# Mixture-of-experts stage: TensorE's program written out row by row, with its first weights addressed in place

## The reference, cut to what matters

```python
# x: layer norm of h, (32 rows, 153 tokens, 192 channels); E = 3 experts, F = 768
scores = softmax(mean(x, axis=1) @ Wg.T)
sel = top_k(scores, 1)                         # one expert per row
h1 = gelu(x @ W1[sel] + b1[sel])               # (153, 768)
y = h1 @ W2[sel] + b2[sel]                     # (153, 192)
out = h + y * scores[sel]
```

## Time and profile before

| | us |
|---|---|
| median of three executions (lowest to highest) | 1019.19 (1018.41 to 1020.95) |
| the profiled execution, its own time | 1023.18 |
| its span, from the first instruction to the last | 1021.4 |
| experts stage, first SyncE entry to the end of the span | 851.3 to 1021.4 |

### The profile page before, as it was taken

How to read it: one execution, slowest core, us unless ns; L and a number is a source line. 1 busy time by engine, 2 the same in 40 slices (tenths; PEclk the granted TensorE clock), 3 DMA queues, 4 the chain that set the end, 5 groups by cost and what they waited for, 6 DMA issues and landing times. The chain is left out here.

```text
span 1021.4 us, 23392 instructions
## 1 busy us (share of the span) xinstructions
PE 705.7 (69%) x6531; PEld 483.7 (47%) x6532; DVE 873.0 (85%) x2391; ACT 708.9 (69%) x1374; POOL 168.2 (16%) x276
## 2 busy tenths in 40 slices
PE   3783387757788376676767667666644386999997
PEld 3562144425555234343434334333323254998996
DVE  5879997988888889999999999999978874676766
ACT  0345365977888789988988998999845293554553
POOL 5851220017664100000000000000004530000000
PEclk9986598988999777878877887788757597999999
DMA  8000000001111111111111111111022004455452
GB/s 260 3 3 0 0 1 1 1 1 40 37 37 37 40 31 25 24 24 24 25 24 24 24 26 24 24 25 24 17 91 75 17 1 155 147 194 193 171 194 82
DMA packets 84274, 54.75 MB, mean 54 GB/s; under 512 B 53704, under 2 KB 83176, under 8 KB 83976
## 3 DMA queue, kind: packets, MB, share of 16 engines
q1 hardware_dynamic: 83208, 54.11, 17.4%
q0 software_dynamic: 1024, 0.13, 0.3%
HBM read 11.90 MB, written 3.76 MB: 15 GB/s over the span
## 5 line engine op out<-in xcount | busy, mean ns | idle before, releaser
L1377 DVE SCALAR_TENSOR_TENSOR expo<-expo,con,pow 128x153 f32<-128x153 f32 x480 | 146.2, 377 | 0.7 <-ACT expo L1287 0.7
L1287 ACT ACTIVATE expo<-at_rem,con 128x459 f32<-128x459 f32 x160 | 98.1, 644 | 14.7 <-PE at_rem L1160 11.2
L962 DVE TENSOR_REDUCE rs_ends<-rs_banks 128x770 f32 (+1 forms) x96 | 89.3, 957 | 12.8 <-PE rs_banks L934 10.6
L784 PE MATMUL at_banks<-pick,row_top 128*128 128x459 bf16 x160 | 73.5, 459 | 37.7 <-ACT word L1250 37.1
L1413 DVE CUSTOM_DVE_ANT_0 weight_top<-weight_top,line 128x2448 uint16<-128x2448 uint16 x64 | 85.6, 1351 | 8.1 <-ACT line L1279 6.3
L1159 PE MATMUL at_rem<-word,ident_half 128*128 128x459 f16 x160 | 64.7, 404 | 37.2 <-ACT expo L1287 34.6
L883 ACT ACTIVATE rs_banks<-rs_banks 128x770 f32<-128x770 f32 x96 | 74.6, 796 | 22.4 <-PE rs_banks L926 21.6
L1243 ACT ACTIVATE pT_all<-at_pT 128x768 bf16<-128x768 int16 (+3 forms) x160 | 79.0, 563 | 13.8 <-PE at_pT L1183 8.3
L1250 ACT ACTIVATE word<-at_banks 128x459 uint8<-128x459 f32 x160 | 79.9, 562 | 9.9 <-PE at_banks L789 8.7
L1943 ACT ACTIVATE qk<-e_p,b1s 128x153 f32<-128x153 f32 x192 | 58.9, 392 | 29.0 <-PE e_p L1904 27.8
L1904 PE MATMUL e_p<-X,qk 128*128 (+1 forms) x960 | 72.9, 236 | 7.7 <-DMA qk<-vt 6.9
(11 more groups left out here) (389 smaller groups left out, 2036.2 us busy)
## 6 DMA issues: line engine op xcount, KB each, us to landing
qk<-vt SPq DMA_DIRECT2D x64, 384.0 KB, 3.1
rs_kb<-qk SPq DMA_DIRECT2D x128, 28.7 KB, 2.0
kb<-qk SPq DMA_DIRECT2D x128, 28.7 KB
patches<-in_patches SPq DMA_DIRECT2D x4, 768.0 KB
vi<-vt SPq DMA_DIRECT2D x32, 96.0 KB, 2.0
out<-vi SPq DMA_DIRECT2D x32, 96.0 KB, 1.8
pj_w<-in_w SPq DMA_DIRECT2D x1, 2304.0 KB, 8.3
qb<-qk SPq DMA_DIRECT2D x128, 6.0 KB
```

The lines of the kernel that those rows point to most:

```text
L784: pe.matmul(bank[:, 0:3 * N], top, pick[:, 3 * i:3 * i + 3, :].rearrange("p w n -> p (w n)"), start=True, stop=False, skip_group_check=True)
L962: v.tensor_reduce(ends[:, :, n, 5 * b:5 * b + 5], banks[:, slot(u, b), :, 0:5 * W].rearrange("p i (t n) -> p i t n", n=W), AX, ALU.max).th ...
L1287: act.activation(bank(ex, b), rem[:, (u + b) % 2, 0:3 * N], ACT.Square, scale=2.0 ** 24, bias=c(5)).then_inc(sq_done, 1)
L1377: ins = v.scalar_tensor_tensor(ex[:, t, :], ex[:, t, :], c(7), pw[:, t, :].bitcast(BF16), ALU.add, ALU.mult, accum_out=tot[:, t:t + 1])
```

## The change

The ring of first weights goes. TensorE's program is written out for all 32 rows, so that the row number is a constant in it; the first product reads `w1h` and `w1l` where they lie, at an address that depends on the expert's register, and the expert number is read one row ahead. SyncE instead copies the expert's low second weight `w2l` (`wl`, a slot of four) and its bias (`bias2`) for each row, and waits for the end of the collect of row n-4 (`i_bias`) before it refills a slot. The image part of the second product is written as six pairs: `w2h` into partitions 0 to 63 of `p3`, `wl` into partitions 64 to 127. VectorE no longer reads the expert number, waits for the row's copies (`w_in`), and has one more addition for the image rows. ScalarE's program, SyncE's and VectorE's loops stay.

```diff
@@ -1828,7 +1828,10 @@
         sb = lambda n, s, t=F32: k.sb(n, s, t, st)
         g = m["qkflat"][:, 12288:12288 + 4 * FT * N].bitcast(F32).rearrange("p (u f n) -> p u f n", u=2, f=FT)
         gs = sb("e_gs", [P, 2, FT, N + 32 + NT], BF16)
-        ws = m["qkflat"][:, 0:SLOTS * 4 * FF].rearrange("p (s i a f) -> p s i a f", s=SLOTS, i=2, a=2)
+        bias2 = m["pj_raw"][:, :, :].rearrange("p a b -> p (a b)")[:, 0:SLOTS * C].rearrange("p (u c) -> p u c", u=SLOTS)
+        wl_own = sb("e_w2_low", [P, 2, FT, C], BF16)
+        wl_line = m["line"][:, :, :].rearrange("p a b -> p (a b)")[:, 2 * FT * B:2 * FT * B + FT * C].bitcast(BF16).rearrange("p (u f c) -> p u f c", u=2, f=FT)
+        wl = [wl_own[:, 0, :, :], wl_own[:, 1, :, :], wl_line[:, 0, :, :], wl_line[:, 1, :, :]]
         rows_out = m["vi"][:, :, :].rearrange("p a b -> p (a b)").bitcast(F32).rearrange("p (t c) -> p t c", c=C)
         share = m["line"][:, :, :].rearrange("p a b -> p (a b)")[:, 0:2 * FT * B].rearrange("p (e f b) -> p e f b", e=2, f=FT)
         yb, ot, yi, oi = rows_out[:, 0:2, :], rows_out[:, 2:6, :], rows_out[:, 6, :], rows_out[:, 7, :]
@@ -1862,9 +1865,9 @@
 
                     e = sp.value_load(sel[0:1, ds(n, 1)], min_val=0, max_val=E - 1)
                     if not (isinstance(n, int) and n < SLOTS):
-                        wait_apart(sp, h_acc, (n - SLOTS) * 2 + 2, k.passed)
-                    for i, w in enumerate((w1h, w1l)):
-                        sp.dma_start(ws[:, u, i, :, :], w[:, :, e, :]).then_inc(w_in[u], 16)
+                        wait_apart(sp, i_bias, n - SLOTS + 3, k.passed)
+                    sp.dma_start(wl[u], w2l[:, e, :, :]).then_inc(w_in[u], 16)
+                    sp.dma_start(bias2[:, u, :], b2[:, e, :]).then_inc(w_in[u], 16)
 
                 def rows(n, j, grp):
                     wait_apart(sp, y_out, n + 2, k.passed)
@@ -1889,24 +1892,24 @@
 
             @block.tensor
             def _(pe):
-                expert = lambda n: pe.value_load(sel[0:1, ds(n, 1)], min_val=0, max_val=E - 1)
-
-                def first_product(n, kk):
+                expert = lambda n: pe.value_load(sel[0:1, n:n + 1], min_val=0, max_val=E - 1)
+
+                def first_product(n, kk, e):
 
                     u = kk % 2
                     pe.wait_ge(h_act, n * FT + FT)
-                    pe.wait_ge(w_in[kk], (n - kk) * 8 + 32)
                     for f in range(FT):
                         o = p1[:, u, f // 3, (f % 3) * N:(f % 3 + 1) * N]
                         fs = slice(f * P, (f + 1) * P)
                         parts = ((0, 0, 0), (1, 0, 0), (0, 0, 1), (0, 1, 2), (1, 1, 2))
                         for a, (w, kt, plane) in enumerate(parts):
-                            mm = pe.matmul(o, ws[:, kk, w, kt, fs], X[:, plane, ds(n * N, N)], start=(a == 0), stop=(a == len(parts) - 1))
+                            mm = pe.matmul(o, (w1h, w1l)[w][:, kt, e, fs], X[:, plane, n * N:(n + 1) * N], start=(a == 0), stop=(a == len(parts) - 1))
                         if f % 3 == 2:
                             mm.then_inc(h_acc, 1)
 
                 def second_product(n, slot, e):
                     pe.wait_ge(g_split, n * 2 + 2)
+                    pe.wait_ge(w_in[slot], (n - slot) * 8 + 32)
 
                     pe.wait_ge(y_bias, n + 1)
                     u = slot % 2
@@ -1915,19 +1918,19 @@
                         mm = pe.matmul(p2[:, u, 0:C], gs[:, u, f, a], w[:, e, f, :], start=(b == 0), stop=(b == 3 * FT - 1))
 
                     wait_apart(pe, i_bias, n + 1, k.passed)
-                    parts = [(w, f) for f in range(FT) for w in (w2h, w2l)]
-                    for b, (w, f) in enumerate(parts):
-                        mm = pe.matmul(p3[0:64, u, 0:C], gs[:, u, f, BOTH], w[:, e, f, :], start=(b == 0), stop=(b == 2 * FT - 1))
+                    for f in range(FT):
+                        pe.matmul(p3[0:64, u, 0:C], gs[:, u, f, BOTH], w2h[:, e, f, :], start=(f == 0), stop=(f == FT - 1))
+                        mm = pe.matmul(p3[64:128, u, 0:C], gs[:, u, f, BOTH], wl[slot][:, f, :], start=(f == 0), stop=(f == FT - 1))
                     mm.then_inc(y_acc, 1)
 
-                def body(c, kk):
-                    now, last = batch(c, kk, 0), batch(c, kk, 1)
-                    e_last = expert(last[0]) if last is not None else None
-                    if now is not None:
-                        first_product(now[0], now[1])
-                    if last is not None:
-                        second_product(last[0], last[1], e_last)
-                steps(pe, body)
+                e_last, e_now = None, expert(0)
+                for n in range(B + 1):
+                    e_next = expert(n + 1) if n + 1 < B else None
+                    if n < B:
+                        first_product(n, n % RING, e_now)
+                    if n > 0:
+                        second_product(n - 1, (n - 1) % RING, e_last)
+                    e_last, e_now = e_now, e_next
 
             @block.scalar
             def _(act):
@@ -1978,18 +1981,20 @@
 
                 def collect(n, j, grp):
                     u, r = j % 2, slice(32 * j, 32 * j + 32)
-                    e = v.value_load(sel[0:1, ds(n, 1)], min_val=0, max_val=E - 1)
                     v.wait_ge(y_acc, n + 1)
+                    v.wait_ge(w_in[j], (n - j) * 8 + 32)
                     v.wait_ge(y_out, n + 1)
-                    v.tensor_tensor(yb[:, u, :], p2[:, u, 0:C], b2[:, e, :], ALU.add).then_inc(y_bias, 1)
+                    v.tensor_tensor(yb[:, u, :], p2[:, u, 0:C], bias2[:, j, :], ALU.add).then_inc(y_bias, 1)
 
                     v.wait_ge(i_out, grp + 1)
-                    v.tensor_tensor(yi[r, :], p3[0:32, u, 0:C], b2[0:32, e, :], ALU.add).then_inc(i_half, 1)
+                    v.tensor_tensor(yi[r, :], p3[0:32, u, 0:C], bias2[0:32, j, :], ALU.add).then_inc(i_half, 1)
                     v.wait_ge(y_bias, n + 3)
                     v.wait_ge(sent[j], (n - j) * 4 + 16)
                     v.scalar_tensor_tensor(ot[:, j, :], yb[:, u, :], gw[:, ds(n, 1)], Hres[:, n, :], ALU.mult, ALU.add).then_inc(y_out, 1)
-                    v.wait_ge(i_half, n + 1)
-                    v.tensor_tensor(yi[r, :], p3[32:64, u, 0:C], yi[r, :], ALU.add).then_inc(i_bias, 1)
+                    v.wait_ge(i_half, n * 2 + 1)
+                    v.tensor_tensor(yi[r, :], p3[32:64, u, 0:C], yi[r, :], ALU.add).then_inc(i_half, 1)
+                    v.wait_ge(i_half, n * 2 + 2)
+                    v.tensor_tensor(yi[r, :], p3[64:96, u, 0:C], yi[r, :], ALU.add).then_inc(i_bias, 1)
 
                 def image(grp):
                     v.wait_ge(i_bias, grp * 4 + 6)
```

## The result

The changed kernel takes 1045.53 us (median of four executions, 1044.90 to 1046.33), the kernel before 1019.35 (1018.41 to 1020.95): a ratio of 1.0255, 95% interval 1.0240 to 1.0269. The change makes the kernel slower by 26 us. The profiled execution took 1045.26 us, its span is 1042.4.

A forecast was written before the change was run, and what follows sets the result against it. The prediction took TensorE's matmuls to bound the kernel before and its program, 5.57 us a row against 4.84, after. Rows +21.9, start -3.4, last row's pairs -0.5 gave +18.0 us: 1041.2 profiled, 1037 median, range 1010 to 1048.

The forecast's parts named there:

- One operation per different address: TensorE's program: each different register-based address costs one register operation, not each matmul or register; 36 a row after the change.
- 0.12 us for one: TensorE's program: price of one register operation, from eleven steps in 1.3 us; 36 of them make 4.32 us a row.
- The open bound: Price of an operation: earlier trace did not settle whether its steps showed the sequencer's own pace; bounds 0.046 and 0.15 us.
- The row, 5.57 us: TensorE's program in a row: operations 4.32, read 0.85, waits 0.30, handing over 0.10 us, against 4.84 now.
- The start, -3.4 us: Start of the experts stage: no weights to wait for, so first matmul at about 853.0 instead of 856.38.
- The difference carries over: Profiled execution to median: the profiled one stays 4.0 us above the median, so 1041.2 becomes 1037.
- The paired image part, worth nothing under the program: Image part of the second product: pairs take 0.50 us off 1.11, but save only 0.5 us, in the last row.
- VectorE, copies, instruction fetch, costed at nothing: Beside TensorE's program: VectorE at most 4.14 us a row, copies with over 14 us of cover, written-out rows: no cost.
- The clock: Experts stage, rival: gaps in the array's work drop the clock to 0.50, 7.5 us a row, about 1095; chance 0.04.
- a chain full of "issue": Profile after, sign of being right: the chain of waits shows mostly "issue" or PE's sequencer, rows 5.5 us apart.
- the 4.14 us for VectorE: VectorE's work in a row: at most 4.84 - 1.15 + 0.35 + 0.1 us after the change.
- the array stays the bound: Experts stage, rival: program runs ahead of the matmuls, pairing counts, row 4.22 us, -22.5 us, 997; chance 0.13.

The follow-up runs named there:

- e5: The changed kernel with twelve more matmuls a row in the first product, at addresses just worked out: 1045.06 us.
- e2: The changed kernel with its image part in turn again and one addition less on VectorE: 1043.46 us.
- e8: The kernel before with the expert's bias copied by SyncE and VectorE without its read of the expert number: 1018.71 us.
- e11: The kernel before with only TensorE's program written out for all rows: 1022.84 us.
- e12: e3 with SyncE's program written out and its weight copies issued one row earlier, ahead of an older row's stores: 1016.11 us.
- e13: e12 with the first weights of rows 0 and 1 read in place, the other thirty rows from the ring: 1011.38 us.
- e15: e13 with the low half of the first weights read in place in every row: 1009.56 us.
- e14: e12 with the image part in turn again: 1018.61 us.
- e6: The changed kernel with TensorE's read of the expert number given no bounds: 1183.04 us.
- e3: The changed kernel with both first-weight halves copied into a ring by SyncE, low second weight and bias copied by GpSimd's queue: 1018.56 us.

## Why the prediction was right

The sign and the mechanism held, and the time lies in the range: 1037 forecast, 1010 to 1048 as the range, 1045.53 measured. The forecast is 8 us short, and nothing cancelled: the rows cost 4.4 us more than foretold, and some 4 us come from the way in which the change was carried from the profiled execution to the median. By its own steps:

- **One operation per different address**: 768 on line 1906, as foretold; e5 shows that matmuls sharing an address add none.
- **0.12 us for one**: 3.0 us over 23 steps is 0.13 in the first product, 1.3 us over 11 steps (945.5 to 946.8) 0.12 in the second. The open bound, that the earlier trace rows might show the matmuls' pace and not the program's, is settled: 24 operations now pace 30 matmuls that need only 2.12 us.
- **The row, 5.57 us**: 5.77. The term that was mis-sized is the first product's 24 operations: 24 x 0.12 = 2.88 foretold, 24 x 0.13 = 3.13 measured. The rest of the row, second product, waits and the read, is 2.64 where 2.69 was foretold. From the first product to the last second product lie 1034.63 - 851.34 = 183.3 us, before 1013.33 - 856.38 = 157.0: 26.3 more, where 21.9 was foretold.
- **The start, -3.4 us**: from TensorE's first read to its first matmul 1.68 us (849.66 to 851.34), 1.7 foretold; the earlier trace rows has 5.1 from SyncE's read. -3.4 as foretold, while the stage itself began 1.7 us earlier in this execution, for no reason in the change.
- **"The difference carries over"**: this failed. The execution profiled before lay 4.0 us above its median, the one profiled after lies at its own: their spans differ by 21.0 us and their times by 22.1, the medians by 26.2. The 1.7 us ahead of the stage are part of that, and no more than the start of the stage moves from one execution to the next: 848.9 to 852.4 us in the fourteen traces, though all that runs before it is the same program. Where the rest of the 4 was, no row shows.
- **The paired image part, worth nothing under the program**: e2. That pairs run side by side holds: in the chain a pair follows a pair after 0.08 us, as one matmul of the text part did (1.49/18). The Trainium skill's rule that a weight load overlaps matmuls in flight only when the row group differs (TensorE: Matmul & The Clock Gate, Part 3, What overlaps and what doesn't) would, as the prediction reads it, have put the two in turn; the trace does not agree.
- **VectorE, copies, instruction fetch, costed at nothing**: no transfer among the waits after; e8 and e11 within 0.3%.
- **The clock**: 1.00 in the window, with gaps in the array's work.
- **One of its signs did not come**: it looked for a chain full of "issue" and for TensorE idle between matmuls. Both are nearly absent, since the recorded matmuls overlap (19.19 of 20 us busy); the count of starts shows what the signs were meant to show.

One rival would not have come out at its price even if its mechanism had held. With a program of 12 operations and pairs the row is 4.63 us (e12, e13), not 4.22. Its sum left out that the read of the expert number stands where the array runs empty, 0.23 us a row, and the 4.14 us for VectorE hold for three rows in four but leave out the image part, with which the fourth takes 4.8. So "the array stays the bound" would have been worth some 1011 here, as e13 shows with its early start, not 997.

## What to carry to other kernels

Matmul operands whose address hangs on a register cost some 0.12 us of TensorE's program here for each different address, however many matmuls use it. Count the addresses of a step and set that sum, with the reads and waits of the program, beside the array's own work: the longer of the two sets the pace (24 were all but free here, 36 cost 1.2 us a row). Even a program that is shorter costs time where it has a long step just as the array runs empty, as the read of the expert number does in e12. A copy to a constant address moves the price of an address to the queues; all copies (e13) and a mix of both (e15), issued ahead of stores that wait, were the fastest and equal within the noise. Give a bound with every number that addresses hang on, and when an engine reads as busy, look at how many instructions it started.

## What the runs showed of the hardware that was not expected

An assertion of 0.018 us costs 0.08 us of TensorE's program, an operation of 0.046 us costs 0.12 to 0.13: the recorded duration is less than two fifths of the price. The same read of one number took 0.31 us in the median in e14 and e15 and 0.61 to 0.62 in e12 and e13, and no run shows why. Twelve further matmuls at addresses already worked out cost nothing (e5). In e6, where the matmuls stood furthest apart, the granted clock averaged 0.76 over the window of 905 to 925 us, so it was at its lower level (0.50, 1.2 GHz) for part of it; in the changed kernel, with 213 matmuls in the same window instead of 120, it stayed at 1.00 (2.4 GHz). In e3 a copy of 384 KB took 5.1 us in the chain at a DMA share of 0.75 (945 to 965 us), 3.1 in the kernel before, whose share is 0.52 in the steady rows.
